# Perceiver block on one core: the maxima of two head groups subtracted by TensorE, their exponents taken in one operation each, and first values in a shared PSUM bank

## The reference, cut to what matters

```python
x = x + cross_attention(ctx, layernorm(x))    # 12544 context rows, 128 queries, softmax over the queries
x = x + self_attention(layernorm(x))          # 16 heads of 16, causal, softmax over 128 keys
x = x + ffn(layernorm(x))                     # 256x256 matrix plus a low-rank correction

# self attention, the part that the change touches:
att = einsum('bhqd,bhkd->bhqk', q, k) / sqrt(hd)
att = where(causal, att, -inf)
att = softmax(att, axis=-1)
y = einsum('bhqk,bhkd->bhqd', att, v)
return einsum('btc,cd->btd', y, w_proj) + b_proj
```

## Time and profile before

| | |
|---|---|
| median of 3 runs | 105.86 us (105.57 to 106.26) |
| the profiled execution's own time | 105.76 us |
| its span, first to last instruction | 103.7 us |
| PE busy in the span | 98.3 us (95%) |
| DVE busy | 76.3 us (74%) |
| ACT busy | 72.7 us (70%) |
| POOL busy | 63.8 us (62%) |
| granted TensorE clock | 0.998 of full |

### The profile page before, as it was taken

The page is one execution under the profiler, slowest core; times in us unless marked ns, Lnnn a source line. Parts: engine busy times, 40 slices in busy tenths (PEclk is TensorE's granted clock), DMA queues, the critical chain, the costliest instruction groups (busy, mean ns, idle before and its releaser), DMA issues.

```text
span 103.7 us, 2257 instructions
## 1 busy us (share of the span) xinstructions
PE 98.3 (95%) x740; PEld 86.4 (83%) x740; DVE 76.3 (74%) x217; ACT 72.7 (70%) x268; POOL 63.8 (62%) x46
## 2 busy tenths in 40 slices
PE   5999999999999999999999999999999999969990
PEld 1389999999999999999999999999998976845660
DVE  0412959959999999988777797777889745699641
ACT  4019599599999999997777977778879304489410
POOL 6405499869999999999766797666886001004020
PEclk9999999999999999999999999999999999999999
DMA  3899999999999999999999999993000000000001
GB/s 70 330 417 412 411 411 406 408 408 408 414 400 409 403 416 406 408 409 409 408 406 406 411 408 409 388 369 125 0 0 6 0 0 0 0 0 0 6 0 51
DMA packets 8746, 27.86 MB, mean 269 GB/s; under 512 B 1120, under 2 KB 1824, under 8 KB 8736
## 3 DMA queue, kind: packets, MB, share of 16 engines
q1 hardware_dynamic: 8736, 27.73, 68.3%
HBM read 27.59 MB, written 0.13 MB: 267 GB/s over the span
## 4 chain that ended last, share of the span: by engine, by line
PE 89%; DVE 4%; DMA 2%; issue 1%; POOL 1%; ACT 0%; DVEq 0%
PE bank L323 43%; PE bank L335 21%; PE bank L338 10%; DVE head_max L716 2%; DMA x<-x_dram 2%; PE bank L406 2%; PE bank L443 1%; PE bank L344 1%; PE bank L419 1%; PE bank L500 1%; PE bank L308 1%; PE bank L486 1%; PE bank L389 1%; PE bank L386 1%; PE bank L462 1%
## 5 line engine op out<-in xcount | busy, mean ns | idle before, releaser
L288 POOL TENSOR_TENSOR rows_split<-rows_ring,rows_split 128x1024 fp32r<-128x1024 f32 (+1 forms) x25 | 58.4, 2335 | 16.9 <-ACT rows_split L518 16.8
L323 PE MATMUL bank<-query_t,cols_ring 128*128 128x128 f32 x392 | 47.5, 276 | 0.0
L323 PEld LDWEIGHTS bank<-query_t,cols_ring 128*128 128x128 f32 x392 | 45.7, 192 | 1.3 <-ACT query_t L509 0.3
L529 ACT ACTIVATE bank<-bank,neg_max 128x128 f32<-128x128 f32 x98 | 33.1, 338 | 7.4 <-DVE neg_max L653 7.2
L335 PE MATMUL bank<-rows_split,probs 128*128 128x512 f32 x92 | 34.7, 413 | 0.0
L518 ACT CAST rows_split<-rows_ring 128x1024 fp32r<-128x1024 f32 (+1 forms) x25 | 25.8, 1033 | 6.1 <-DMA rows_ring<-ctx_rows_dram 5.1
L670 DVE SCALAR_TENSOR_TENSOR probs<-bank,inv_sums,probs 128x128 fp32r<-128x128 f32 x98 | 27.6, 345 | 0.9
L338 PE MATMUL bank<-rows_split,probs 128*128 128x256 f32 x92 | 25.6, 279 | 0.0
L653 DVE TENSOR_REDUCE neg_max<-bank 128x4 f32<-128x512 f32 (+1 forms) x25 | 16.8, 672 | 8.6 <-PE bank L323 8.6
L335 PEld LDWEIGHTS bank<-rows_split,probs 128*128 128x128 f32 x92 | 17.3, 189 | 3.1
L529 ACT ACTIVATION_READ_ACCUMULATOR bank<-bank,neg_max 128x1 f32 x98 | 19.8, 202 | 0.0
(11 more groups left out here) (96 smaller groups left out, 64.0 us busy)
## 6 DMA issues: line engine op xcount, KB each, us to landing
cols_ring<-ctx_cols_dram SPq DMA_DIRECT2D x24, 512.0 KB, 14.8
rows_ring<-ctx_rows_dram SPq DMA_DIRECT2D x24, 512.0 KB, 15.2
wqk_sb<-w_qk_dram SPq DMA_DIRECT2D x1, 512.0 KB, 11.6
cols_ring<-ctx_cols_dram SPq DMA_DIRECT2D x1, 256.0 KB, 11.3
rows_ring<-ctx_rows_dram SPq DMA_DIRECT2D x1, 256.0 KB, 12.1
wv_sb<-w_v_dram SPq DMA_DIRECT2D x1, 256.0 KB, 11.7
wproj_sb<-w_proj_dram SPq DMA_DIRECT2D x1, 256.0 KB, 10.4
wffn_sb<-w_ffn_dram SPq DMA_DIRECT2D x1, 256.0 KB, 9.7
```

The lines of the kernel that those rows point to most:

```text
L288: pool.tensor_tensor(rows_split[:, b, 0:n, 1, :], rows_ring[:, slot * STEP:slot * STEP + n, :], rows_split[:, b, 0:n, 0, :].bitcast(F32), ...
L323: last = pe.matmul(into[:, t * P:(t + 1) * P], cols_ring[:, slot * STEP + t, c, :], query_t[:, c, :], start=(c == 0), stop=(c == DC - 1))
L529: last = act.activation(on[:, t * P:(t + 1) * P], on[:, t * P:(t + 1) * P], ACT.Exp, bias=neg_max[:, b, t:t + 1], accum_out=sums[:, b, t:t ...
```

## The change

A new PE function `shift_scores(j)` multiplies the identity (float32) by `head_max[:, j]` spread over 128 columns a head, and accumulates that into the bank `head_scores[j]`: one matmul of 128x512. It is used for groups 1 and 3. ACT then takes the exponents of the whole group straight from PSUM in one operation. The tile `shifted` and DVE's subtraction go away. Group 3 is no longer taken head by head, so its sums are made by DVE in one reduction of 128x512. The halves of turn 3 go away: one `turn_exps(3)` into bank 5, one copy by ACT. The copy of inverse 0 moves from DVE to ACT, between the copies of turns 2 and 3. `y_t_ps[0]` moves to bank 2, beside `x2_ps`, and the values of group 0 come ahead of the `x1_bias` matmul, since they now open the bank. `y_t_ps[1]` moves to bank 3. The inverse transpose 0 moves ahead of the values of group 1.

```diff
--- before.py
+++ after.py
@@ -107,7 +107,6 @@
         bq_scaled = sb("bq_scaled", [P, DC])
         v_pad = sb("v_pad", [P, DC, 2, HM, 32])
         head_max = sb("head_max", [P, GROUPS, HM])
-        shifted = sb("shifted", [P, HM, P])
         head_exp = sb("head_exp", [P, GROUPS, HM, P])
         folded = sb("folded", [P, HM, P // 2])
         head_exp_t = sb("head_exp_t", [P, GROUPS, HM, P])
@@ -133,10 +132,9 @@
         head_scores = [bank[0], bank[1], bank[3], bank[4]]
         low_rank_ps = bank[7]
         k_ps, q_ps, v_ps = [bank[2], bank[6]], [bank[5], bank[7]], bank[2]
-        exp_t_ps = [bank[5], bank[0], bank[1]]
-        exp_t_ends = [bank[5], bank[0]]
+        exp_t_ps = [bank[5], bank[0], bank[1], bank[5]]
         inv_ps = [bank[7][:, P:2 * P], bank[6][:, P:2 * P]]
-        y_t_ps = [bank[3], bank[4]]
+        y_t_ps = [bank[2][:, D:D + P], bank[3]]
         x2_ps, x2_t_ps, ffn_ps = bank[2], [bank[7], bank[6]], bank[1]
 
 
@@ -179,13 +177,11 @@
         v_copied = sem("v_copied")
         head_scores_ready = sem("head_scores_ready")
         head_max_ready = sem("head_max_ready")
-        shifted_ready = sem("shifted_ready")
+        scores_shifted = sem("scores_shifted")
         head_exp_ready = sem("head_exp_ready")
-        head_exp_half = sem("head_exp_half")
         fold_step = sem("fold_step")
         exp_turned = sem("exp_turned")
         exp_t_copied = [sem(f"exp_t_copied{j}") for j in range(GROUPS)]
-        exp_t_copied_end = sem("exp_t_copied_end")
         y_summed = sem("y_summed")
         head_inv_ready = sem("head_inv_ready")
         inv_spread = sem("inv_spread")
@@ -429,6 +425,8 @@
             def turn_exps(j):
 
                 pe.wait_ge(head_exp_ready, j + 1)
+                if j == GROUPS - 1:
+                    pe.wait_ge(exp_t_copied[0], 1)
                 for m in range(HM):
                     last = pe.transpose(exp_t_ps[j][:, m * P:(m + 1) * P], head_exp[:, j, m, :], ident[:])
                 last.then_inc(exp_turned, 1)
@@ -437,8 +435,6 @@
                 c, e = j // 2, j % 2
 
                 pe.wait_ge(exp_t_copied[j], 1)
-                if j == GROUPS - 1:
-                    pe.wait_ge(exp_t_copied_end, 1)
                 for m in range(HM):
                     last = pe.matmul(y_t_ps[c][32 * m:32 * m + 32, 0:P], v_pad[:, c, e, m, :],
                                      head_exp_t[:, j, m, :], start=(e == 0), stop=(e == 1), skip_group_check=True)
@@ -450,29 +446,24 @@
                 pe.matmul(inv_ps[c], head_inv_wide[:, c].rearrange("p m e d -> p (m e d)"), ident[:],
                           start=False, stop=True, is_transpose=True, skip_group_check=True).then_inc(inv_spread, 1)
 
-            def turn_end(h):
-
-                if h == 0:
-                    pe.wait_ge(exp_t_copied[0], 1)
-                    pe.wait_ge(head_exp_half, 1)
-                else:
-                    pe.wait_ge(exp_t_copied[1], 1)
-                    pe.wait_ge(head_exp_ready, GROUPS)
-                for m in range(2):
-                    last = pe.transpose(exp_t_ends[h][:, m * P:(m + 1) * P], head_exp[:, GROUPS - 1, 2 * h + m, :],
-                                        ident[:])
-                last.then_inc(exp_turned, 1)
-
+            def shift_scores(j):
+
+                pe.wait_ge(head_max_ready, j + 1)
+                pe.matmul(head_scores[j][:], ident[:], head_max[:, j, :].unsqueeze(2).to_broadcast([P, HM, P]),
+                          start=False, stop=True, skip_group_check=True).then_inc(scores_shifted, 1)
+
+            shift_scores(1)
             turn_exps(0)
             turn_exps(1)
+            shift_scores(3)
             pe.wait_ge(v_copied, 2)
-            pe.matmul(x2_ps[:, 0:D], ident[:], x1_bias[:], start=True, stop=False, skip_group_check=True)
+            pe.wait_ge(exp_t_copied[0], 1)
+            weigh_values(0)
+            pe.matmul(x2_ps[:, 0:D], ident[:], x1_bias[:], start=False, stop=False, skip_group_check=True)
             turn_exps(2)
-            weigh_values(0)
-            turn_end(0)
+            spread_inverse(0)
             weigh_values(1)
-            turn_end(1)
-            spread_inverse(0)
+            turn_exps(3)
             spread_inverse(1)
             weigh_values(2)
             weigh_values(3)
@@ -573,14 +564,15 @@
                 for m in range(HM):
                     last = act.activation(head_exp[:, j, m, :], head_scores[j][:, m * P:(m + 1) * P], ACT.Exp,
                                           bias=head_max[:, j, m:m + 1], accum_out=head_sums[:, j // 2, j % 2, m:m + 1])
-                    if j == GROUPS - 1 and m == 1:
-                        last.then_inc(head_exp_half, 1)
                 last.then_inc(head_exp_ready, 1)
 
             def exps_shifted(j):
 
-                act.wait_ge(shifted_ready, 1)
-                act.activation(head_exp[:, j], shifted[:], ACT.Exp).then_inc(head_exp_ready, 1)
+                act.wait_ge(scores_shifted, j // 2 + 1)
+                act.activation(head_exp[:, j], by_head(head_scores[j]), ACT.Exp).then_inc(head_exp_ready, 1)
+
+            def by_head(tile):
+                return tile[:].rearrange("p (m k) -> p m k", k=P)
 
             def copy_exp_t(j):
                 act.wait_ge(exp_turned, j + 1)
@@ -590,11 +582,11 @@
             exps_by_head(0)
             exps_shifted(1)
             exps_by_head(2)
-            exps_by_head(3)
+            exps_shifted(3)
             copy_exp_t(2)
-            act.wait_ge(exp_turned, GROUPS + 1)
-            act.copy(head_exp_t[:, GROUPS - 1, 2:HM].rearrange("p m q -> p (m q)"), exp_t_ends[1][:, 0:2 * P])\
-               .then_inc(exp_t_copied_end, 1)
+            act.wait_ge(inv_spread, 1)
+            act.copy(inv_t[:, 0, :], inv_ps[0]).then_inc(inv_copied, 1)
+            copy_exp_t(3)
             act.wait_ge(inv_spread, DC)
             act.copy(inv_t[:, DC - 1, :], inv_ps[DC - 1]).then_inc(inv_copied_end, 1)
             for c in range(DC):
@@ -725,14 +717,8 @@
                 dve.wait_ge(y_summed, 2 * c + 2)
                 dve.tensor_tensor(y_t[:, c, :], y_t_ps[c][:, 0:P], inv_t[:, c, :], ALU.mult).then_inc(y_t_ready, 1)
 
-            maximum_of_heads(0)
-            maximum_of_heads(1)
-            dve.wait_ge(head_max_ready, 2)
-            dve.tensor_tensor(shifted[:], by_head(head_scores[1]),
-                              head_max[:, 1, :].unsqueeze(2).to_broadcast([P, HM, P]),
-                              ALU.add).then_inc(shifted_ready, 1)
-            maximum_of_heads(2)
-            maximum_of_heads(3)
+            for j in range(GROUPS):
+                maximum_of_heads(j)
             dve.wait_ge(v_ready, 1)
             dve.wait_ge(pads_ready, 1)
             v_view = v_ps[:, 0:D].rearrange("p (c e m d) -> p c e m d", c=DC, e=2, d=HD)
@@ -748,12 +734,8 @@
             link(dve.tensor_reduce(head_sums[:, 0, 1, :], folded[:, :, 0:P // 4], AX_X, ALU.add))
             invert_sums(0)
             dve.wait_ge(head_exp_ready, GROUPS)
+            link(dve.tensor_reduce(head_sums[:, 1, 1, :], head_exp[:, GROUPS - 1], AX_X, ALU.add))
             invert_sums(1)
-            dve.wait_ge(exp_turned, GROUPS)
-            dve.tensor_copy(head_exp_t[:, GROUPS - 1, 0:2].rearrange("p m q -> p (m q)"), exp_t_ends[0][:, 0:2 * P])\
-               .then_inc(exp_t_copied[GROUPS - 1], 1)
-            dve.wait_ge(inv_spread, 1)
-            dve.tensor_copy(inv_t[:, 0, :], inv_ps[0]).then_inc(inv_copied, 1)
             dve.wait_ge(inv_copied, 1)
             finish_y(0)
             dve.wait_ge(inv_copied_end, 1)
```

## The result

The changed kernel takes 106.81 us (median of 7 runs, 106.68 to 107.02) where the kernel before takes 106.13 (7 runs, 105.57 to 106.27): a ratio of 1.0076, 95% interval 1.0054 to 1.0097. That is 0.7 us slower by the medians and 0.8 us by the ratio, clear of the noise, and within 1%. A later set of runs gave 1.0089 (1.0058 to 1.0120). The forecast was 107.0, in a range of 106.2 to 107.7.

What follows compares the result with a forecast made beforehand. It took DVE to set the end up to 94.13 us and PE's queue from 94.17. Following PE's starts put the last values +1.16 us later: 106.92 us for the profiled execution, 107.02 by the median, forecast 107.0, range 106.2 to 107.7.

Steps and rivals of the forecast that it cites:

- What bounds the stretch: DVE sets the chain from 90.53 to 94.13 us, then PE to 97.80, busy for all of 3.63 us.
- The price of a shift: On PE, a float32 matmul of 512 columns takes 1.13 us, between bounds of 0.384 and 1.40.
- Group 1 is late: The first shift ends at 92.98, so ACT's exponents start at 93.01 and turn 1 at 93.70, 0.38 us later.
- Group 3's saving on ACT is not had: ACT's group 3 falls from 1.39 to 0.64 us but waits for the second shift, ending at 95.98 against 96.06.
- The copy in one piece: ACT copies all of turn 3 in 0.63 us while PE idles for part; adds 0.25 us in the bulk check.
- The sum: PE's queue followed start by start puts the last values at 98.54 against 97.38: +1.16 us.
- The cross-check in bulk: On PE's stretch, 1.06 us added for a shift, 0.15 off for the split turn, 0.25 for the copy: about +1.16.
- the cheap shift: Rival: a shift's 512 columns take PE only 0.384 us, giving +0.2 us, 106.1 us; chance 0.16 for 106.1 to 106.6.
- The dear shift: Rival: each shift takes PE 1.40 us and both lie on the path, +1.7 us, 107.5 us; chance 0.11.
- the one in which nothing comes of it: Rival: ACT's shorter group 3 balances PE's longer queue, +0.5 us, 106.4 us; counted with the cheap shift's 0.16.
- The one in which DVE counts: Rival: 0.60 us less on DVE moves PE's stretch up, ending 0.6 us earlier at 105.2 us; chance 0.08.
- only swaps two terms: On PE, the changed order of values 0 and x1_bias was counted as merely exchanging two terms.

Runs made afterwards that it cites:

- the bf16 trial: The changed kernel with both shifts in bf16 instead of float32; ratio 1.0019 against the kernel before, first maximum to first projection +0.16 us.
- shared bank alone: The kernel before with only the first values moved to bank 2, ahead of x1_bias and turn 2, no PE shift; ratio 1.0033 against the kernel before.
- version of all findings: The changed kernel with bf16 shifts, x1_bias in PE's gap, values 0 ahead of turn 2, turn 3 in halves copied by ACT; ratios 0.9979, 0.9958 against before.
- the split copy: The changed kernel with turn 3 in two banks, its halves copied by DVE and ACT; ratios 1.0105 and 1.0071 against the kernel before.

## Why the prediction was right, point by point

**What bounds the stretch.** Right for the changed kernel: with 0.6 us more on DVE the stretch is the same, so DVE's relief was no reserve. For the kernel before it was read off PE's 3.63 us of 3.63, and that reading is too simple. Turn 2 waited there for ACT as well (94.67 to 94.72), which the prediction did not name, and by that path the first shift alone cost 0.34 us. No run takes work off DVE alone in the kernel before.

**The price of a shift.** Right in size. From an idle PE it lands after 1.13 to 1.14 us, the pair of 256 columns that I took. The records start 0.43 us apart for the second shift. Neither bound was near: not 0.384, not 1.40. A maximum repeated 128 times took no longer than the pair of 256 columns did. The prediction quotes a sustained 131 ns per matmul of 512 columns from the Trainium skill, page "TensorE: Matmul & The Clock Gate", section "Back-to-back issue gap", and estimates from it that the sum would be some 0.6 us shorter. The trace does not show such a rate: the shift's float32 records of 512 columns start 0.43 us apart.

**Group 1 is late.** Right. Exponents 1 start 2.51 us after the first maximum begins (2.50 forecast), turn 1 3.16 (3.19). Alone, that part costs 0.34 us.

**Group 3's saving on ACT is not had.** Right. Its exponents end at 95.99, 5.31 us after the first maximum; before, it was 5.55. That is 0.16 us sooner than the forecast 5.47, as the second shift and the exponents were shorter. They are ready 1.2 us ahead of turn 3 (97.17). Only DVE's sum starts on them at once (96.03), and its inverse, ready at 97.21, is not turned until 97.67.

**The copy in one piece.** Right that PE waits for it: the weight loads stand idle for 0.48 us ahead of the last values. The wait of PE itself is 0.21:

```profile
98.50 0.42 PE L439 MATMUL bank<-head_exp_t,v_pad 128*32 128x128 f32 x8 [0.21 <-ACT head_exp_t L579]
```

**The sum.** It gave +1.16 us; the stretch shows +0.95. The absolute times hid this: I had 98.54 for the last values and the trace has 98.50, but there the stretch began 0.17 us later than in the trace of before. The agreement of the totals, 107.0 forecast and 106.81 measured, is in part luck: the forecast started from a median of 105.86 us, and in the runs of the result the kernel before had 106.13. From that, +1.16 would have been 107.29. The change itself was 0.7 to 0.8 us by the time. The term mis-sized most is the second shift. I took 1.13 us for it too, with its weight load in the open. It stands behind transposes with full arrays, and lasts 1.02:

```profile
94.33 1.02 PE L452 MATMUL bank<-head_max,ident 128*128 128x512 f32 x2
```

That is 0.11 of the 0.21. The rest are three pieces of 0.04: exponents from PSUM at 0.60 where I had 0.64, the copy at 0.59 where I had 0.63, and turn 2 up to the inverse, 0.44 where I had 0.48; within rounding that is the 0.21. The cross-check in bulk was no independent support: its rows give 0.13 for the split turn (twice 0.36 less 0.59) where it has 0.15.

**The chances.** I gave slower by over 1% the most (0.53), and within 1% 0.44. It came out at 0.76%, and 0.89% in the second set. By the median my sum was 107.02, 0.10 us over the threshold of 106.92; with the 0.21 us taken off it is 106.81, just under it. So the mechanism and the direction were right, and the class that I held likeliest was not.

**Of the rivals**, the cheap shift is what the bf16 trial became: +0.2 was forecast, +0.16 measured in the stretch. The dear shift fell with 1.13 us for its 1.40, and so did the one in which nothing comes of it, +0.5 against +0.95 in the stretch. The one in which DVE counts fell too, for the changed kernel. What I missed in the part on the order of PE's queue is that to put the first values ahead of x1_bias "only swaps two terms": alone it costs 0.47 us, and it is free in the changed kernel only because the second shift covers it.

## What to carry to other kernels

When work moves from an engine that seems to be the bottleneck to one with a gap, ask of the result, not of the engine, when it comes: the first shift ran in PE's gap and still cost 0.34 us, because DVE had delivered sooner (ACT began group 1 at 2.12 us of the stretch, now at 2.51). Then follow the receiving engine's queue to the end with the distances between starts that its own trace shows; here that gave each start to about 0.2 us, with errors that add up along the queue (0.03 at turn 1, 0.21 at the last values). An operand that only has to be the same in numerator and denominator, as the maximum of a softmax, can be subtracted in bf16 at a third of the price, and that, with independent work put in the remaining gap and the queue in another order, turned the loss into a gain.

## What the runs showed that I had not expected

- Exponents of 128x512 from PSUM took 0.598 us in the changed kernel, less than the 0.641 of the same operation from SBUF. That is not shown to be the memory's doing. In all traces such an operation of ACT took 0.60 us as exponents and 0.58 to 0.59 as a copy where ACT had waited before it, and 0.61 to 0.64 where it came right behind another one. The 0.641 from SBUF stood right behind group 0's. In the kernel with bf16 shifts the exponents from PSUM stand right behind others too, and took 0.613 and 0.644. So two of the three pieces of 0.04 in the sum were prices taken from rows of ACT at work, for operations that now begin after a wait.
- In three kernels (bf16 shifts, shared bank alone, version of all findings) the first values start 0.14 us after DVE's copy of turn 0 ends, in the split copy the last ones 0.15 us after ACT's, where other steps to PE took 0.04 to 0.05. What makes them longer is open.
- The first maximum begins at different times in two traces of one kernel, 91.00 and 90.30 us, which is more than most differences looked for here. A difference of a few tenths in such a kernel is to be read between two points of one trace.
